# Two attentions' rows multiplied in their last item, a norm's statistics one step ahead, clearing in pieces, one item loaded ahead

## The reference

```python
x = L0_attn_x                                    # (4, 1024, 128)
x = x + ln(attn0(ln(x), Wqkv, Wout))             # 16 heads of 8, scores clipped to +-10, causal
x = x + ln(ffn0(ln(x), ...))                     # latent attention (16 heads of 64) + mixture of 8 experts, top 2
x = x + ln(attn1(ln(x), w_qkv))                  # 16 heads of 8, causal softmax with a maximum
x = x + ln(ffn1(ln(x), U1, V1, b1, U2, V2, b2))  # rank 32: gelu(x U1 V1 + b1) U2 V2 + b2
```

## Time and profile before

| what | us |
|---|---|
| three runs | 2028.51 (median), 2027.21, 2033.88 |
| the profiled execution, its own time | 2033.21 |
| its span from first to last instruction | 2031.4 |
| first projection | 0 to 69.8 |
| first attention (16 items) | 69.8 to 368.1 |
| first joining stage | 368.1 to 485.3 |
| latent attention, its finish, experts | 485.3 to 1392 |
| second projection | 1392 to 1453.9 |
| second attention | 1453.9 to 1919.8 |
| last stage | 1919.8 to 2031.4 |

### The profile page before, as it was taken

One profiled execution on the slowest core, in us unless ns is written; L12 is line 12 of the kernel. 1 busy time (PEld: TensorE's weight loads), 2 busy tenths in 40 slices (PEclk: granted clock), 3 DMA queues, 4 the chain that ended last, 5 costly groups with the idle time before them and its releaser, 6 DMA issues. The chain is left out here.

```text
span 2031.4 us, 41380 instructions
## 1 busy us (share of the span) xinstructions
PE 1731.9 (85%) x12312; PEld 712.3 (35%) x12312; DVE 1299.7 (64%) x2419; ACT 1139.6 (56%) x1786; POOL 666.0 (33%) x1222
## 2 busy tenths in 40 slices
PE   5787788687899999999999869996599899899777
PEld 3311112343333434434333544444233233233232
DVE  6578888463766666656662335555588788788154
ACT  6599999341055545545556333324257677677645
POOL 6355555574222312212221011104222222222254
PEclk9799999798799999989999979998799999999988
DMA  7532234357112213213210400001622112122201
GB/s 220 126 64 63 56 55 113 86 139 152 27 38 53 60 39 63 49 39 64 49 38 22 162 14 1 0 0 56 155 43 44 43 32 46 46 46 62 55 12 42
DMA packets 91731, 125.80 MB, mean 62 GB/s; under 512 B 24497, under 2 KB 63793, under 8 KB 91330
## 3 DMA queue, kind: packets, MB, share of 16 engines
q1 hardware_dynamic: 91554, 123.51, 25.9%
HBM read 75.77 MB, written 47.58 MB: 61 GB/s over the span
## 5 line engine op out<-in xcount | busy, mean ns | idle before, releaser
L1036 ACT ACTIVATE q_buf<-ps 128x1024 f32<-128x1024 f32 (+1 forms) x1152 | 863.5, 822 | 526.9 <-PE ps L920 525.4
L1138 DVE TENSOR_REDUCE o_sb<-ps 128x1 f32<-128x512 f32 (+3 forms) x864 | 718.0, 865 | 280.9 <-PE ps L949 187.0
L1096 POOL TENSOR_SCALAR_AFFINE_SELECT q_buf<-q_buf 128x256 f32<-128x256 f32 x768 | 363.3, 498 | 826.2 <-ACT q_buf L1036 680.2
L969 PE MATMUL ps<-q_buf,v_buf 128*9 128x512 f32 (+7 forms) x4608 | 462.9, 497 | 55.7 <-POOL q_buf L1096 53.1
L920 PE MATMUL ps<-q_buf,k_buf 49*128 49x512 f32 (+3 forms) x1536 | 325.1, 524 | 5.9 <-issue 5.9
L920 PE MATMUL ps<-q_buf 48*128 48x512 bf16 (+7 forms) x1536 | 259.9, 333 | 51.6 <-ACT q_buf L1036 30.4
L1198 DVE TENSOR_SCALAR q_buf<-q_buf 128x1024 f32<-128x1024 f32 x288 | 214.6, 753 | 57.1 <-ACT q_buf L1036 52.5
L920 PEld LDWEIGHTS ps<-q_buf 48*128 48x128 bf16 (+1 forms) x1536 | 76.2, 94 | 303.6 <-ACT q_buf L1036 231.6
L920 PEld LDWEIGHTS ps<-q_buf,k_buf 49*128 49x128 f32 x1536 | 133.0, 190 | 136.4 <-ACT q_buf L1036 66.8
L969 PEld LDWEIGHTS ps<-q_buf,v_buf 128*9 128x9 f32 (+1 forms) x4608 | 92.4, 96 | 232.2 <-issue 121.5
L942 PE MATMUL ps<-k_buf,q_buf 48*128 48x512 bf16 (+3 forms) x768 | 116.1, 335 | 19.3 <-DVE o_sb L1138 12.8
(11 more groups left out here) (172 smaller groups left out, 1625.3 us busy)
## 6 DMA issues: line engine op xcount, KB each, us to landing
q_buf<-qm_d SPq DMA_DIRECT2D x32, 384.0 KB, 6.7
qm_d<-pr_buf SPq DMA_DIRECT2D x80, 128.0 KB, 2.4
o_d<-pr_buf SPq DMA_DIRECT2D x16, 512.0 KB, 2.7
q_buf<-o_d SPq DMA_DIRECT2D x8, 1024.0 KB, 5.1
q_d<-q_buf SPq DMA_DIRECT2D x48, 128.0 KB, 2.1
k_d<-q_buf SPq DMA_DIRECT2D x48, 128.0 KB, 1.9
q_buf<-q_d SPq DMA_DIRECT2D x64, 96.0 KB
q_buf<-k_d SPq DMA_DIRECT2D x64, 96.0 KB
```

What stands on the lines that cost most here:

```text
L969: mm = nc.tensor.matmul(ps[VW * j:VW * j + V_ROWS_OUT, o_bank + half % O_BUFS, lo * P:(lo + nq) * P], v, units(i, r, j)[:, 0, off * P:(off ...
L1036: nc.scalar.activation(units(i, g, WIDE * e, WIDE), ps[:, bank:bank + WIDE, :], ACT.Exp, scale=scale).then_inc(s_e, 1)
L1096: nc.gpsimd.affine_select(out=blk, in_=blk, compare_op=ALU.is_ge, fill=0.0, base=0, pattern=[[0, 2], [1, P]], channel_multiplier=-1)\
L1138: nc.vector.tensor_reduce(to, sc, AX_X, ALU.max).then_inc(s_mr, 1)
```

## The change

1. The clearing of L512 becomes eight pieces of 1024 columns, one behind each of the first projection's chunks on VectorE.
2. Only item 0 is loaded at the end of a projection; item 1's loads are issued by SP at the start of the attention, once item 0 has landed.
3. In both attentions the reciprocals are at rows 0, 2 and 4 of item 14, and the spread is issued in item 14 instead of 15, in the second attention before that item's `maxima`. In item 15 POOL waits behind row 2's selections for the spread and multiplies chunks 0 to 3; at the end it multiplies chunks 4 and 5. Only chunks 6 and 7 (`LATE` = 6) are left for the next stage.
4. In the first joining stage `inverse_rms` is one chunk further ahead and stands between the second and third join; VectorE's addition and second statistics stand before the second product.
5. In the last stage the second norm's statistics and inverse are of chunk c+3 instead of c+2, POOL's addition comes first in a step, and VectorE's apply comes before the statistics.

```diff
--- before.py
+++ after.py
@@ -79,7 +79,7 @@
         phase_sems = []
-        ahead_item = [nc.alloc_semaphore(name=f"ahead_item{n}") for n in range(2)]
+        ahead_item = nc.alloc_semaphore(name="ahead_item")
@@ -508,8 +508,6 @@
-                    if first:
-                        nc.vector.memset(area[32:64, 0:8192], 0.0)
                     for c in range(4):
@@ -533,6 +531,8 @@
                             stats(c + 4)
+                        if first and c < 8:
+                            nc.vector.memset(area[32:64, 1024 * c:1024 * (c + 1)], 0.0)
                     if first:
@@ -646,10 +646,9 @@
                                     parts[:, c % PR, s, part, :]).then_inc(s_st[c % PR], 16)
-                    for r in range(2):
+                    for r in range(HALVES):
                         sp.wait_ge(s_st[r], 16 * 7)
-                    for n in range(2):
-                        load_item8(sp, 0, n, n, n, ahead_item[n])
+                    load_item8(sp, 0, 0, 0, 0, ahead_item)
                     for r in range(PR):
@@ -663,6 +662,8 @@
             sp.dma_start(o_rows[:, b, :], o8_d[b].rearrange("h d t -> (h d) t")).then_inc(done, 16)
+
+        LATE = CHUNKS - HALVES
@@ -835,9 +836,9 @@
                         else:
-                            for s in range(2):
-                                sp.wait_ge(ahead_item[s], 16 * n_loads * (1 if clip else 2))
-                                sp.sem_inc(s_ld[s], 16 * n_loads)
+                            sp.wait_ge(ahead_item, 16 * n_loads * (1 if clip else 2))
+                            sp.sem_inc(s_ld[0], 16 * n_loads)
+                            load(0, 0, 1)
                         if has_max:
@@ -856,7 +857,7 @@
                             load_sums()
-                        if not latent and last == ITEMS - 1:
+                        if not latent and last == ITEMS - 2:
                             spread_inverses()
@@ -1096,6 +1097,10 @@
                                         .then_inc(s_sel, 1)
+                            if not latent and last == ITEMS - 1 and g == 2:
+                                pool.wait_ge(s_rows, 16 * (EARLY + 8))
+                                for c in range(4):
+                                    multiply_rows(c)
                             if latent and g == 2 and (last is None or last + 2 < ITEMS):
@@ -1112,8 +1117,7 @@
                         if not latent:
-                            pool.wait_ge(s_rows, 16 * (EARLY + 8))
-                            for c in range(HALVES):
+                            for c in range(4, LATE):
                                 multiply_rows(c)
@@ -1179,7 +1183,7 @@
-                    INVERSIONS = (3, 5, 7) if clip else (0, 1, 2)
+                    INVERSIONS = (0, 2, 4)
@@ -1188,7 +1192,7 @@
                         for g in range(ROWS_P):
-                            if not latent and last == ITEMS - (2 if clip else 1) and g in INVERSIONS:
+                            if not latent and last == ITEMS - 2 and g in INVERSIONS:
                                 invert(INVERSIONS.index(g))
@@ -1224,8 +1228,7 @@
-            if c >= CHUNKS - HALVES:
-                pool.wait_ge(s_rows, 16 * 9)
+            pool.wait_ge(s_rows, 16 * 9)
             multiply_rows(c).then_inc(s_mul, 1)
@@ -1336,8 +1339,8 @@
                     def out_projection(c):
-                        if c >= HALVES:
-                            pe.wait_ge(s_mul, c - HALVES + 1)
+                        if c >= LATE:
+                            pe.wait_ge(s_mul, c - LATE + 1)
                         if c > 0:
@@ -1483,17 +1486,18 @@
                     for c in STEPS:
-                        if there(c + 1):
-                            inverse_rms(c + 1)
                         if there(c + 2):
...
                             join(c, 1)
+                        if there(c + 2):
+                            inverse_rms(c + 2)
+                        if there(c):
                             join(c, 2)
                             join(c, 3)
-                        if HALVES <= c + 4 < CHUNKS:
-                            multiply_later(pool, c + 4, s_rows, s_mul)
+                        if c in (1, 2):
+                            multiply_later(pool, LATE + c - 1, s_rows, s_mul)
@@ -1551,10 +1555,11 @@
                             copy_values(c)
-                            products_q(c, 1)
                         if there(c + 2):
...
                             stats2(c + 2)
+                        if there(c):
+                            products_q(c, 1)
@@ -2111,16 +2116,16 @@
                     for c in STEPS:
+                        if there(c + 3):
+                            add(c + 3)
                         if there(c + 4):
                             norm1.inverse(pool, c + 4)
-                        if there(c + 2):
-                            norm2.inverse(pool, c + 2)
+                        if there(c + 3):
+                            norm2.inverse(pool, c + 3)
                         if there(c - 2):
                             norm3.inverse(pool, c - 2)
-                        if there(c + 3):
-                            add(c + 3)
-                        if HALVES <= c + 5 < CHUNKS:
-                            multiply_later(pool, c + 5, s_rows, s_mul)
+                        if c in (0, 1):
+                            multiply_later(pool, LATE + c, s_rows, s_mul)
@@ -2145,14 +2150,14 @@
                         if there(c + 2):
-                            dve.wait_ge(s_x1, c + 3)
-                            norm2.stats(dve, c + 2, tiles(x_res, c + 2))
-                        if there(c - 3):
-                            add(c - 3)
-                        if there(c + 2):
                             if c + 2 > 1:
...
                             norm2.apply(dve, c + 2, tiles(x_res, c + 2), xn[:, (c + 2) % 2, :, :])
+                        if there(c + 3):
+                            dve.wait_ge(s_x1, c + 4)
+                            norm2.stats(dve, c + 3, tiles(x_res, c + 3))
+                        if there(c - 3):
+                            add(c - 3)
                         if there(c - 1):
```

## The result

Twenty executions of the changed kernel had a median of 2017.83 us (2006.27 to 2026.94), twenty of the kernel before 2030.08 us (2023.37 to 2043.55). The two medians lie 12.3 us apart. The ratio of the two sets of runs is estimated as 0.9926, with a 95% interval of 0.9909 to 0.9944: 15 us faster, between 11 and 18. The forecast was 33 us, 1995, with a range of 1983 to 2013. The sign was right, the size wrong, and the median lies outside the range.

A forecast was written before the change was run, and what follows sets the result against it. Nine stages run in series; the two joining stages were taken as bound by chains of short instructions between engines. Terms -3.8 - 4.4 - 5.1 + 2.4 - 8.7 + 4.5 - 18 = -33.1 took 2028.5 to 1995.4 us, range 1983 to 2013.

The forecast's parts named there:

- Clearing in pieces: First projection's start: pieces lie in VectorE's idle time and all moves 3.8 us ahead; -3.8 us (-2.5 to -4.5).
- One item ahead: Ends of both projections: 13 fewer loads issued before the barrier; -4.4 us in the first, -5.1 in the second.
- some 2 us behind its last issue: End of first projection: item 0 lands this late, so about 0.7 us of the 5.1 us gain is lost.
- First attention: Last items: VectorE's clips and POOL's four new multiplications exclude each other; +2.4 us (0 to +5).
- First joining stage: New order shortens the cycle to about 10.4 us, seven steps from 80.8 to 72.1; -8.7 us (-4 to -11).
- Second attention: Last two items: maxima queue behind the spread on SP, PE stalls 3.7 us, plus 0.8 for clock; +4.5 (0 to +8).
- After a gap of 4.16 us PE's granted clock was 0.50 for 9.6 us, so I add 0.8: Second attention, item 15: the clock's price after the 3.7 us stall, put at 0.8 us.
- Last stage: Second norm's apply no longer waits; start 9 us sooner, seven steps 59.5 to 48.2; -18 us (-8 to -22).
- rival (a): Last stage gives only 8 us, first joining stage 4, as another handed-over wait is late next; 2010 us, chance 0.18.
- rival (b): Last stage runs at PE's lower clock throughout, +24 where -18 was forecast; 2037 us, slower, chance 0.04.

The follow-up runs named there:

- rows_at_end: The changed kernel with the four multiplications of item 15 put back behind the last item in both attentions; 2015.82 us, ratio 0.9928 to the kernel before.
- rows_only: The kernel before with multiplications moved into the attentions' last item and the spread into item 14 behind the maxima, old starts and orders; 2029.98 us, ratio 1.0007.
- rows_kept: two_mended without the moved multiplications: these and the spread stay where they were in the kernel before; 2006.53 us, ratio 0.9884 to the kernel before.
- maxima_first: The changed kernel with item 15's maxima stored and loaded before the spread on SP in the second attention; 2002.44 us, ratio 0.9867 to the kernel before.
- two_mended: maxima_first with the third norm's inverse before the second norm's on POOL in the last stage; 1997.09 us, ratio 0.9818 to the kernel before.

## Why the prediction was wrong, point by point

- **Clearing in pieces**, -3.8: right. The first statistics begin at 5.65 (forecast 5.7); a piece takes 0.91 us and lies in idle time.
- **One item ahead**: second projection -5.1 as forecast. In the first, clearing and loads together gave 6.2 instead of 8.2. The failed step is "some 2 us behind its last issue": landing took 4.4 us (59.11 to 63.53). In the kernel before it was hidden behind item 1's issue, and no row showed it. The Trainium skill (DMA: Bandwidth & Descriptors, Anatomy of one DMA — SWDGE (gpsimd) path) gives about 2.0 us as the fixed part of one DMA issued from GpSimd. These loads are issued from SP, so that figure isn't theirs, and the last of thirteen took 4.4.
- **First attention**, +2.4: the mechanism is shown and costs 1.5. The stage still took 298.2 to 300.0, as before (298.3), since the profile before had falls of the clock of about that size in it (rows_at_end reached its last copy 2.1 us earlier than the kernel before).
- **First joining stage**, -8.7: -10.1 to -10.4. Seven steps took 71.9 us (second products at 389.17 and 461.04), 72.1 were forecast, and the single steps came nearly as forecast (10.0, two of 11.9, 10.7, 11.0, 8.4 and 8.0 us); the rest came at the two ends. That moving the multiplications matters only with the new order is what rows_only and rows_kept show.
- **Second attention**, +4.5: this is the term that failed. The queue on SP, the late landing and the stall were right in place and in size (3.7 forecast, 4.0 to 4.9 measured). The step "After a gap of 4.16 us PE's granted clock was 0.50 for 9.6 us, so I add 0.8" was not. It took one fall's length as the length of all falls, and gave no working for the 0.8: in its own row PE is busy for all of the 9.60 us, so at full clock that work would take half as long. The clock stayed at 0.50 for 27.3 and 37.5 us, and this cost 7.5 and 11.1 us. Stall and clock together cost 11.5 and 16.0 us in the two profiles, and 12.0 to 12.6 by the ratios of maxima_first, where 4.5 was forecast. Of the 18 us that are missing, this is 7 to 11.5. It is an error of the change, mended by exchanging two calls.
- **Last stage**, -18: -16.1, the applies and the first steps as forecast (first copy 29.8 us after the stage's start, before 39.8). The seven steps took 53.4 us where 48.2 were forecast: 6.8 and 6.6 where 7.8 each was forecast, then one of 13.0. This is rival (a) in small: the third norm's inverse, last of three on POOL, is late once, and the clock turned 1.4 us into 5. With that mended (two_mended) they take 48.1, but from steps of 6.8, 6.6, 8.1, 8.8, 6.8, 6.6 and 4.4: that the sum agrees is luck in part.
- **What was in no term**: the experts, 5 us longer in both profiles of the changed kernel.
- **The sum** by what was measured: -6.2, 0, -10.2, -5.1, +15 (mean of the two profiles), -16.1, +5.4 in the experts: -17, where the ratio says -15 (-11 to -18). The range failed because it took +8 as the worst end of the second attention and nothing for the clock elsewhere; rival (b) had the clock as a risk of the last stage alone. The ends of its terms add up to -48 and -9, not to -50 and -5, so what was measured lies between them; the range that was drawn, 1983 to 2013, was narrower.

## What to carry to other kernels

A stall of PE is not paid with its own length: here a stall of 4.7 to 4.9 us brought 7.5 to 12 us of slower matmuls behind it, and a gap of 3.1 us another 2 to 3.5. So give every new wait on PE's path two prices, and cover a gap that can't be avoided with filler, or exchange what stands on the queue ahead of it. When a move puts DMAs on a queue, look at the shortest hand-over that uses the same queue next. And move work off a ring only when the ring is what ends the step: the same multiplications were worth nothing in one order and about 8 us at one clock in the other.

## What the runs showed of the hardware

- With a gap of 4.7 to 4.9 us the granted clock went to its lower level (1.2 GHz) inside the gap and stayed there for 27.3 to 37.5 us, while PE worked for most of that time (21.24 of 27.31 us, 31.06 of 37.54). After the gap of 4.16 us in the earlier trace rows it was 9.6 us. With gaps of 3.1 us it was 7 to 10 us, and after 1.69 us it didn't fall at once.
- The length of the gap alone doesn't give the length of the fall. At the start of the last stage of the kernel before PE had stood for 5.30 us, then did a transposition and filler matmuls, and the clock was at 0.50 for 3.4 us only (timeline, then windows of that stretch and the next):

```profile
1920.17 1.11 PE L2003 MATMUL ps<-identity,q_buf 128*128 128x128 f32 x4 [5.30 <-POOL q_buf L2112]
...
1919.86:1923.27 3.41, 3.10 (x7) 1.92 (x8) 1.27 (x8) 0.00 (x0) 0.67 (x3) 0.50 0.56 145
1923.27:1950.58 27.31, 19.11 (x62) 8.33 (x61) 12.95 (x49) 9.19 (x20) 16.18 (x24) 1.00 0.09 26
```

- The same matmuls in the same stage had 0.91 in two programs and 0.88 to 0.90 in twelve, so a single profile of this kernel carries several us of clock in stages that nobody touched.
- The last of thirteen small loads issued in 5 us from one queue landed 4.4 us after its issue ended; with the issues divided over two queues it was 3.5 us.
